# A row of 48 small bf16 products, once in six groups, in the cosine passes of a four-layer graph network

## The reference

```python
def _agnn_layer(h, src, dst, beta, n_nodes):
    norm = jnp.sqrt(jnp.sum(h * h, axis=-1, keepdims=True))
    nh = h / jnp.maximum(norm, EPS)
    cos = jnp.sum(nh[src] * nh[dst], axis=-1)
    e = beta * cos
    m = jax.ops.segment_max(e, dst, num_segments=n_nodes)
    ee = jnp.exp(e - m[dst])
    den = jax.ops.segment_sum(ee, dst, num_segments=n_nodes)
    p = ee / den[dst]
    out = jax.ops.segment_sum(h[src] * p[:, None], dst, num_segments=n_nodes)
    return jax.nn.relu(out)
```

## Time and profile before

| | |
|---|---|
| median of 3 runs | 16194.08 us (16192.64 to 16202.92) |
| span of the profiled execution, first to last instruction | 16122.9 us |
| the median less this span | 71.2 us |
| busy: GpSimd, TensorE, VectorE, ScalarE | 9426.9, 7118.7, 6491.8, 2663.4 us |
| mean granted clock of TensorE | 0.503 |
| passes 1 and 2 | 5289 to 11200 us |

### The profile page before, as it was taken

The page is one execution under the profiler, slowest core; times in us unless marked ns, Lnnn a source line. Parts: engine busy times, 40 slices in busy tenths (PEclk is TensorE's granted clock), DMA queues, the critical chain, the costliest instruction groups (busy, mean ns, idle before and its releaser), DMA issues.

```text
span 16122.9 us, 152937 instructions
## 1 busy us (share of the span) xinstructions
PE 7118.7 (44%) x35085; PEld 6087.1 (38%) x35140; DVE 6491.8 (40%) x18639; ACT 2663.4 (17%) x7299; POOL 9426.9 (58%) x9933
## 2 busy tenths in 40 slices
PE   4311111232332566666656666665444444333333
PEld 1100001222222565666656566665333333233333
DVE  3322224333333455555555555554333333222222
ACT  0000000000000333333433333333000000000000
POOL 4476673666666555555545555554666665666666
PEclk5555555555555555555555555555555555555555
DMA  1000001111111111111121121112112122111111
GB/s 29 3 5 5 4 5 43 22 22 22 22 22 22 34 38 40 39 39 41 38 38 44 45 46 44 44 44 38 39 42 43 41 43 47 28 24 24 23 24 23
DMA packets 429662, 499.75 MB, mean 31 GB/s; under 512 B 235856, under 2 KB 245584, under 8 KB 417584
## 3 DMA queue, kind: packets, MB, share of 16 engines
q0 software_dynamic: 317504, 279.59, 11.9%
q1 hardware_dynamic: 97730, 214.09, 3.9%
q10 hardware_dynamic: 14316, 4.81, 0.2%
HBM read 397.49 MB, written 94.54 MB: 31 GB/s over the span
## 4 chain that ended last, share of the span: by engine, by line
DVE 27%; another core or an unknown queue 24%; issue 23%; DVEq 19%; PE 6%; SPq 0%; POOL 0%; ACT 0%; DMA 0%; ACTq 0%; POOLq 0%
DVEq L1371 7%; DVE pay_d L1371 6%; DVE pay_d L1221 5%; DVEq L420 4%; DVE ps L1170 2%; DVE ps L1161 2%; DVE pd L1103 2%; DVE prod L1156 1%; DVE Z L1149 1%; DVEq L1221 1%; PE ps L1568 1%; PE ps L1581 1%; DVE Z L1146 1%; DVE Z L1209 1%
## 5 line engine op out<-in xcount | busy, mean ns | idle before, releaser
L685 POOL DMA_INDIRECT Z<-table,idx x4986 | 4717.0, 946 | 3913.4 <-issue 1662.4
L1581 PE MATMUL ps<-Z 128*128 128x65 f32 x9972 | 2330.5, 416 | 4323.2 <-DVE Z L1209 1546.2
L1581 PEld LDWEIGHTS ps<-Z 128*128 128x128 f32 x9972 | 2203.3, 328 | 4562.5 <-issue 4417.2
L685 POOL DMA_INDIRECT Z<-table_a,idx x1662 | 1572.0, 946 | 945.2 <-issue 557.7
L661 POOL DMA_INDIRECT bins_dst<-slot_d x1612 | 1562.7, 969 | 960.8 <-issue 493.2
L685 POOL DMA_INDIRECT Z<-table_b,idx x1662 | 1571.9, 946 | 854.0 <-issue 535.0
L1371 DVE SCALAR_TENSOR_TENSOR pay_d<-pay_d,ps 128x65 f32 x4986 | 1111.2, 223 | 2365.7 <-issue 1884.6
L1568 PE MATMUL ps<-Z 128*128 128x65 f32 x6648 | 1528.1, 417 | 176.6 <-DVE pay_d L1221 113.7
L1535 PE MATMUL ps<-pay_d,Z 128*128 x6648 | 1535.9, 421 | 62.0 <-ACT Z L744 37.5
L1568 PEld LDWEIGHTS ps<-Z 128*128 128x128 f32 x6648 | 1475.7, 332 | 231.4 <-DVE pay_d L1221 110.9
L1535 PEld LDWEIGHTS ps<-pay_d,Z 128*128 128x128 f32 x6648 | 1486.5, 333 | 64.2 <-issue 63.9
(11 more groups left out here) (245 smaller groups left out, 7970.7 us busy)
## 6 DMA issues: line engine op xcount, KB each, us to landing
pay_d<-locals_ SPq DMA_DIRECT2D x92, 1152.0 KB
Z<-table,idx POOLq DMA_INDIRECT x4986
table_b<-pay_d SPq DMA_DIRECT2D x192, 256.0 KB
Z<-table_a,idx POOLq DMA_INDIRECT x1662
Z<-table_b,idx POOLq DMA_INDIRECT x1662
bins_dst<-slot_d POOLq DMA_INDIRECT x1612
table_a<-kept SPq DMA_DIRECT2D x94, 256.0 KB
slot_d<-pay_d SPq DMA_DIRECT2D x62, 91.0 KB
```

What stands on the lines that cost most here:

```text
L685: nc.gpsimd.indirect_dma_start(rows[:, at.slot, j, 0:width], None, ps_.table, bass.IndirectOffsetOnAxis(ap=idx[:, at.slot, j:j + 1], axis= ...
L1581: last = mm(p_pair[:, at.three, j * ROW:(j + 1) * ROW], hot_d[:, at.three, j, :], given, start=True, stop=True)
```

## The change

A view `p_warm` is laid over the last 128 columns of both banks of `p_row`, which nothing else uses. In `rows_of_destinations`, for groups in slot 0 of the ring of six, TensorE first issues 48 products of 128 columns in bf16 into it: the negative identity is loaded as weights each time, the first 128 columns of `w_parts` are streamed, and none of them raises a semaphore. The wait for `multiplied` is moved ahead of them, and so ahead of the wait for `hot_32_made`. Both cosine passes run this code; the other passes don't.

```diff
+WARMING = 48
...
+        p_warm = prow[:, :, ITEMS * D:512]
...
                 def rows_of_destinations(at):
 
+                    pe.wait_ge(multiplied, done(e + at.g - 2))
+                    if at.slot == 0:
+                        for _ in range(WARMING):
+                            mm(p_warm[:, at.two, :], less_ident_b[:, :], w_parts[:, 0, 0:P], start=True, stop=True)
                     pe.wait_ge(hot_32_made, done(e + at.g))
-                    pe.wait_ge(multiplied, done(e + at.g - 2))
                     for j in range(ITEMS):
```

## The result

The changed kernel takes **16353.84 us** (16339.98 to 16367.21, 4 runs), the kernel before, beside it on the same chip, 16198.5 us: ratio 1.0094, 95% interval 1.0079 to 1.0108, 155 us slower. The forecast was 460 us slower.

A forecast was written before the change was run, and what follows sets the result against it. Bound: TensorE's reports, held back while fetches are in flight, with about 32 products allowed out unreported. Row delays +540 us and clock -80 us give +460 us on 16194.08: 16654 us, own range 16490 to 16808, 8 in 10 16150 to 16850.

The forecast's parts named there:

- the held-back reports: Cosine passes: while fetches are in flight, TensorE's reports are held back and come together some 2.3 us after the last fetch.
- The limit of about 32: TensorE: about 32 products may be out without a report, so a row of 48 breaks into pieces.
- my four places: Groups 76 and 82 of both cosine passes, worked out singly: the row delays VectorE by 5.0, 7.2, 7.4 and 3.4 us.
- The moved wait: TensorE's wait for VectorE's multiply, moved ahead of the row: costs nothing, being over before it is reached.
- The row itself, 5.3 us: TensorE time of 48 products at 0.11 us each, at 1.2 GHz; 94 rows take 498 us.
- the delay is passed on: Each row's delay, 5.75 us on the mean, reaches GpSimd's next fetches unabsorbed: 94 rows give +540 us.
- The clock: A raised granted clock speeds the 24 fp32 products behind the row: -80 us, bounds nothing and -244 us.
- One in three: Share of the 94 broken rows taken to raise the granted clock, giving -80 us.
- 2.6 us where it rises: Time the 24 fp32 products behind a row save when the granted clock rises.
- rival 2: Clock stays up over most of six groups, fp32 products behind spreads take 2.8 us less: 15944 us; chance 0.15.
- Rival 1: Row fills TensorE's idle time, limit not of products: +160 us, 16354; chance 0.14, plus 0.09 that the clock offsets it.
- Rival 3: Knock-on: rows push half their groups' reports into the next run of fetches, 7.5 us each: 17090 us; chance 0.05.

The follow-up runs named there:

- the first chip: Chip of the main measurement: changed kernel with 48-product rows against the kernel before (16198.5 us), 16353.84 us, ratio 1.0094.
- B: Chip where before takes 15959.91 us: changed kernel 16397.93 us (1.0277), row of 24 products instead of 48 16087.12 us (1.0078).
- D: Chip, before 15959.71 us; ratios to it: changed kernel 1.0260, 48 products of one partition 1.0261, 48 of one column 1.0207, row of 24 1.0074.
- E: Chip, before 16145.25 us; ratios to it: wait moved without row 1.0004, two rows of 24 1.0100, 24 of one column 1.0113, 12 fp32 products 1.0059.
- A: Chip, before 12804.58 us; ratios to it: wait moved without row 0.9999, 48 of one column 1.0046, 12 fp32 products 1.0179, 48 of one partition 1.0191.
- C: Chip, before 12819.19 us; ratios to it: changed kernel 1.0009, 48 of one partition 1.0188, 48 of one column 1.0045, 12 fp32 products 1.0179.

## Why the prediction was right and wrong

**What bounds the kernel, and the held-back reports: right on the first chip, and on B, D and E**, with about 16000 us each. Not a property of the kernel: on A and C it doesn't happen.

**The limit of about 32: right, but it doesn't bite everywhere.** On B and D rows of 48 are broken in 83 of 94 places, nearly all after 24 to 31 products; on the first chip 19 are whole and the others break after 1 to 29; on C none is broken. Rows of 24 go out whole in 87 to 90 places of 94 on B and D, and in 144 of 186 on E. 48 products without work cost 340 us. By my four places those of one column would delay 3.1, 5.9, 6.1 and 0.1 us (each remaining product at 0.03 instead of 0.11 us), 3.8 on the mean and 357 us; measured 340, which in the light of chip E is in part luck. The number itself is read from the traces, 32 in the earlier trace rows; on D 46 of the 83 stops in a row come with 31 to 36 products unreported by the trace's marks and none with fewer; where it shows more, marks may be missing. What sets it, no run shows.

**The moved wait: right**, 0.9999 and 1.0004.

**The row itself, 5.3 us: right at the low clock**, 5.0 us for the row of one partition on A and C. The 1.2 GHz beside it no run shows; the runs show a granted clock of 0.50 and 0.107 us from start to start. That the row's own products get faster where the clock rises inside it was left out of the sum: on C the real row takes 3.7 to 4.1 us. There its products start 0.056 us apart behind the rise.

**The step that failed is "the delay is passed on", with its reason, that "no later fetch was waiting to take it up"**, the term of 540 us. On the first chip the whole change cost 155 us, 1.65 a row, though a single place was even later than computed (7.4 us in group 76, against 5.0). The distance with the row in it did grow by 4.7 and 2.5 us, but the other five of each six gave back 2.4 and 2.0. Over 94 rows that is some 200 us taken back, most of the 305 us that the forecast had too many. The waits that shrank are the one ahead of the maxima in pass 1 (652.1 to 429.3 us) and, in pass 2, just one that the sentence said wasn't there: GpSimd's for ScalarE's indices (432.7 to 82.8 us). Also, I let every row break, and of these 94 rows 19 are whole. I worked four groups out as if the ones behind stayed as they were. They don't: where reports come in bursts, a row shifts the length of all six groups. Without the clock the delay is 432 us on D, 4.6 us a row, so there most of it was passed on; the failure is of the first chip above all, and why the two differ is open.

**The clock: mis-sized.** "One in three" was too low for the rises, 91 of 94. For what the sum needs, a high clock at the fp32 products, it is 49 of 94 on the first chip and 16 on D. "2.6 us where it rises" looks right by C's mean, 222/94 = 2.36 us, but that is luck: it is 4.8 us in pass 2 and nothing in pass 1. Where the row is broken the rise is spent inside it: on D the medians differ by 14 us, against my 80. On the first chip the rows took 9.2 and 6.7 us (pass 1, 2) against 12.3 and 10.4 on D, and 19 instead of 11 were whole; its 12 products of line 1540 are faster than on D, so the clock probably gave back more there, but no row without its clock ran beside it and its size is not measured. What I set against rival 2, that the clock falls in a pause (before, behind the earlier trace rows, 13593.3 to 13606.9 us: 0.50, with TensorE busy for 0.55 us of 13.6), happened inside the row: on D it fell before the row's last product in 66 of its 85 rises.

**Rival 1** (16354, "hidden after all") has the number of the result and not its reason: the row isn't hidden, most are broken as in the forecast, and that the number agrees to the microsecond is chance. Its mechanism is the one of pass 1 on A and C, where the row costs nothing. **Rival 3**, no sign of it. **Rival 2**: on C the row raises the clock every time, but for 10.1 us only, and the time comes out 18 us above before.

**What stays open.** Why reports are held back on some chips and not on others. Why before takes 15960 us on B and D and 16145 to 16198 on E and the first, while the changed kernel takes 16354 to 16398 on all three where it ran; the difference between +155 and +438 lies mostly in this, and no profile of the kernel without a row was taken on B or D. How the 305 us too many of the first chip divide between the delay and the clock. And why 12 fp32 products cost less than 24 of one column. No version here beats before.

## What to carry to other kernels

Filler work for TensorE had two prices here, its time and its number: ahead of reports that come late, 48 products of 1.3 us cost 3.6 us a row (chip D). Whether its time costs anything depends on who waits at the place: on chip A 48 products of one partition cost nothing in pass 1 and all of their time, 245 us, in pass 2 of the same kernel. The burst meant to raise the clock gave 222 us back on C, where all 94 rows went out in one piece right ahead of the work that was to gain, and nothing that the runs can tell on D, where 83 of 94 were broken; count what can be out before you place one, and compare it with the same burst without the clock (here operands of one partition, 0.503). And a delay worked out at single groups was too high in every case here where groups wait in bursts (540 us worked out against 432 and less); try it on more than one chip before its size is believed.

## What the runs showed of the hardware

- The same kernel takes 12804 to 12819 us on two chips and 15960 to 16198 on the others. Of the 3322 us between the profiled spans of the first chip and A, 1650 lie between the first and the last group maxima, where A shows no "remote" wait ahead of the maxima and the first chip 652.1 us of them in 2600 of pass 1. 988 us lie ahead of the cosine passes and 684 behind; what makes those is open.
- While a row is stuck its products leave singly or a few together, mostly 0.7, 1.4 or 2.1 us apart (after, B and D).
- 48 products of 128 columns with operands of one partition, 5.0 us in one piece, leave the granted clock at 0.50; those with 128 partitions, whose values differ as well, raise it every time on C (94 of 94). Neither did 12 fp32 products of 128 partitions, 4.9 us long, raise it (0.503 on A, C and E).
